# Layer-norm rows on ScalarE, mask operands padded to 128 rows, and 18 first-pass products moved between the down products of a two-FFN attention kernel

## What is computed

```python
x = x + 0.5 * _L0_ffn_ref(_layernorm(x), ...)
x = x + _L0_attn_ref(_layernorm(x), ...)
x = x + 0.5 * _L0_ffn_ref(_layernorm(x), ...)
```

## Time and profile before

| | us |
|---|---|
| median of 3 runs | 827.32 (825.87 to 828.84) |
| the profiled execution, its own time | 826.89 |
| its span, first to last instruction | 824.9 |
| PE busy | 753.1 (91%) |
| DVE busy | 592.5 (72%) |
| ACT busy | 431.5 (52%) |
| POOL busy | 69.7 (8%) |

### The profile page before, as it was taken

The page is one execution under the profiler, slowest core; times in us unless marked ns, Lnnn a source line. Parts: engine busy times, 40 slices in busy tenths (PEclk is TensorE's granted clock), DMA queues, the critical chain, the costliest instruction groups (busy, mean ns, idle before and its releaser), DMA issues.

```text
span 824.9 us, 15805 instructions
## 1 busy us (share of the span) xinstructions
PE 753.1 (91%) x5508; PEld 329.2 (40%) x5508; DVE 592.5 (72%) x1913; ACT 431.5 (52%) x626; POOL 69.7 (8%) x83
## 2 busy tenths in 40 slices
PE   3979998775799999999999999999998879899998
PEld 2623333332234344444444444444443655233343
DVE  4875332777899999999999999999993377433301
ACT  3432323333337687676876768767677434223211
POOL 2200000444400000000000000000000021000000
PEclk9979999999769999999999999999999989699999
DMA  4201000153401010110101101011000000000012
GB/s 128 67 0 15 0 1 0 49 160 95 133 13 34 20 34 18 34 35 22 32 18 35 34 21 32 18 35 35 22 14 2 1 1 1 0 1 0 0 39 64
DMA packets 33068, 26.08 MB, mean 32 GB/s; under 512 B 5707, under 2 KB 32331, under 8 KB 32997
## 3 DMA queue, kind: packets, MB, share of 16 engines
q1 hardware_dynamic: 32996, 25.15, 10.7%
HBM read 14.62 MB, written 10.26 MB: 30 GB/s over the span
## 4 chain that ended last, share of the span: by engine, by line
PE 63%; DVE 19%; issue 12%; ACT 3%; POOL 1%; SPq 0%; DMA 0%; DVEq 0%; ACTq 0%; POOLq 0%
PE ps L964 57%; DVE mx L853 8%; PE ps L969 5%; DVE xn L659 3%; DVE mx L846 1%; ACT h_all L580 1%; POOL rstd L421 1%; DVE stats L647 1%; PE ps L1012 1%; DVE x L802 1%; DVE h_all L846 1%; DVE mv L651 1%; DMA x<-in_x 0%; SPq L310 0%; DVE wb L874 0%
## 5 line engine op out<-in xcount | busy, mean ns | idle before, releaser
L580 ACT ACTIVATE h_all<-ps 128x1024 f32<-128x1024 f32 (+3 forms) x384 | 291.1, 811 | 118.4 <-PE ps L964 115.0
L853 DVE TENSOR_REDUCE mx<-ps 128x1 f32<-128x512 f32 (+2 forms) x352 | 222.6, 681 | 8.5 <-PE ps L964 5.9
L964 PE MATMUL ps<-ks,xnT_all 57*128 57x512 bf16 (+3 forms) x768 | 180.3, 336 | 10.7 <-DVE mx L846 5.3
L964 PE MATMUL ps<-h_all,vb 128*32 128x512 f32 (+3 forms) x1536 | 163.0, 498 | 0.6 <-ACT osb L569 0.6
L964 PE MATMUL ps<-xnT_all,ks 59*128 59x512 bf16 (+3 forms) x768 | 158.4, 330 | 3.7 <-ACT h_all L580 3.4
L846 DVE CUSTOM_DVE_ANT_0 h_all<-ps,mask_w 128x384 bf16<-128x384 f32 (+1 forms) x256 | 148.9, 618 | 2.1 <-issue 0.3
L670 DVE TENSOR_TENSOR h_all<-ps,sg 128x512 f32<-128x512 f32 (+1 forms) x80 | 55.1, 689 | 107.9 <-PE ps L964 71.3
L964 PEld LDWEIGHTS ps<-ks,xnT_all 57*128 57x128 bf16 x768 | 56.7, 94 | 141.3 <-DVE mx L846 66.1
L964 PE MATMUL ps<-cb 64*128 64x64 bf16 (+3 forms) x1216 | 111.8, 214 | 0.0
L495 ACT ACTIVATE sg<-ps 128x512 f32<-128x512 f32 x80 | 47.6, 598 | 106.3 <-PE ps L964 106.3
L964 PEld LDWEIGHTS ps<-cb 64*128 64x128 bf16 x1216 | 79.8, 96 | 16.7 <-issue 0.3
(11 more groups left out here) (123 smaller groups left out, 627.3 us busy)
## 6 DMA issues: line engine op xcount, KB each, us to landing
xnT_all<-q_scr SPq DMA_DIRECT2D x64, 96.0 KB
q_scr<-qp SPq DMA_DIRECT2D x8, 384.0 KB, 2.7
ks<-k_scr SPq DMA_DIRECT2D x64, 48.0 KB
x<-in_x SPq DMA_DIRECT2D x8, 256.0 KB, 2.9
q_scr<-qp SPq DMA_DIRECT2D x8, 256.0 KB, 2.9
out<-x SPq DMA_DIRECT2D x8, 256.0 KB, 2.3
xnT_all<-bias_scr SPq DMA_DIRECT2D x64, 18.0 KB
q_scr<-qp SPq DMA_DIRECT2D x8, 128.0 KB, 2.3
```

Source lines behind the costliest of these rows:

```text
L580: act.activation(pr[:, (NSTEP * i + s) % PR_BUFS, p:HPG:SLOTS, lo:HALF], ps[:, b:b + 2, lo:HALF], ACT.Exp)\
L853: dve.tensor_reduce(m, src, AX.X, V.max).then_inc(a_out, 1)
L964: return pe.matmul(o, l, r, start=start, stop=stop, skip_group_check=True)
```

## The change

What it does, by place:

- **Loads.** Group loads of x have a semaphore each and no longer wait for one another; group 1 goes ahead of the weights. `ident`, `gate_w`, `lb`, `rank` are issued from ACT's queue; the masks, `esel`, slopes and `qpos` are loaded behind x, ACT's copies of them (`constants`) run in front 6, and `slope_parts` behind `choose`.
- **Rows on ACT.** DVE only makes `shift` = -mean x rstd (one small operation, `ln_shift`); ACT applies scale and shift to the four tiles, in both FFNs' fronts and in the down stage. The copy into `xnT` in the fronts is gone.
- **Shared products.** Those of groups 4 to 7 are taken out of the fronts and put behind them, before the routed tiles; their `hidden` stand inside `choose`. The first `mask_T` stands ahead of the first two gate and up products.
- **Mask operands.** `esel` and `maskT` have 128 rows, 120 of them zero.
- **Down stage of the first FFN.** Banks: y 7, both turns 3, V 4, Q 5, K 6, and 0 to 2 for the ring. V is made directly with tokens on the rows (four products, bias on DVE); K comes as four products into one 128x128 block, and its split moves from POOL to DVE. `v_T` is gone. `EARLY` puts 2 first-pass products behind group 3's projection, and for groups 4 to 7 two before the last down product and two behind the projection: 18 in all. Group 7's split (`last_split`) is put behind product 21 of the first pass.
- **Stores.** k is stored by one DMA for each part and row: nine DMAs in place of six for each group. The first stack is loaded behind group 0's store, the first maxima ahead of group 7's.
- **Loops** over groups are written out on all engines.

The diff, cut to its core (`...` marks what is left out):

```diff
+EARLY = [(0, 0), (0, 0), (0, 0), (0, 2), (2, 2), (2, 2), (2, 2), (2, 2)]
+EARLY_END = sum(map(sum, EARLY))
+LAST_SPLIT = EARLY_END + 4
...
-def over_groups(eng, body):
...
+def over_groups(body):
+    for c in range(GROUPS):
+        body(c, c % 2, c == 0, c == GROUPS - 1)
...
-        esel = sb("esel", [EXPERTS, MT * P], BF16)
+        esel = sb("esel", [P, MT * P], BF16)
-        maskT = sb("maskT", [EXPERTS, 2, GN], BF16)
+        maskT = sb("maskT", [P, 2, GN], BF16)
...
+            sp.dma_start(xt(0), xd[0]).then_inc(s_x[0], 16)
+            sp.dma_start(xt(1), xd[1]).then_inc(s_x[1], 16)
             load(ffn_loads, s_w)
+            for c in range(2, GROUPS):
+                sp.dma_start(xt(c), xd[c]).then_inc(s_x[c], 16)
+            load(const_loads, s_const)
...
+                    for m in range(products):
+                        sp.dma_start(k_scr[b, :, r + m, n].rearrange("k (t n) -> t k n", t=GT), kp[:, par, m])\
+                            .then_inc(dw, 16)
...
+            def ln_apply(c, par, s_nm, s_T, s_xn):
+                act.wait_ge(s_nm, c + 1)
+                after(act, s_T, c)
+                for t in range(GT):
+                    ins = act.activation(xn[:, t, :], x[:, c * GT + t, :], ACT.Identity, bias=shift[:, par, t:t + 1],
+                                         scale=rstd[:, par, t:t + 1])
+                ins.then_inc(s_xn, 1)
...
                     act.activation(xnT_all[:, c, :], bank(7 * par), copy).then_inc(f.xA, 1)
-                    if not first:
+                    if not last:
+                        ln_apply(c + 1, 1 - par, f.nm, f.T, f.xn)
+                    if 0 < c <= LATE_SHARED:
                         silu(c - 1, 1 - par)
+                    if load_constants and c == GROUPS - 2:
+                        constants()
...
+                    act.activation(kp[:, par, 0, :], ps[:, 6, 0:P], ACT.Identity, bias=bk[:, 0:1])
+                    act.activation(kf[:, :], ps[:, 6, 0:P], ACT.Identity, bias=bk[:, 0:1]).then_inc(f.kf, 1)
...
+                dve.scalar_tensor_tensor(out=shift[:, par, :], in0=mv[:, par, :, 0], scalar=-1.0, in1=rstd[:, par, :],
+                                         op0=V.mult, op1=V.mult).then_inc(s_nm, 1)
...
+                    shared(LATE_SHARED)
+                    shared(LATE_SHARED + 1)
                     first_max(s2, m2, r2, pick2)
...
                     mask(0, 0)
+                    for c in range(LATE_SHARED + 2, GROUPS):
+                        shared(c)
...
                         ln_stats(c, par, ch, f.ve2)
-                        ln_apply(c, par, f.rs2, f.Tb, f.xn2)
+                        early_maxima(early(c, 0))
+                        ln_shift(c, par, f.rs2, f.xn2, f.nm2)
                         if not first:
                             split(c - 1, 1 - par)
+                            values(c - 1, (c - 1) // 2, 1 - par)
+                        early_maxima(early(c, 1))
...
+                def down(c, par, transpose=False):
+                    after(pe, f.yT, c if qkv else c - 1)
                     for i in range(HT):
                         if transpose and i == HT // 2 + 1:
                             xn_T(c - 2)
+                        if transpose and i == HT - 1:
+                            early_pieces(early(c - 1, 0))
...
                     mm(bank(5), wq[:, :], xnT[:, par, :]).then_inc(f.Q, 1)
+                    for t in range(GT):
+                        ins = mm(ps[:, 4, w * t:w * t + w], xnT[:, par, t * P:(t + 1) * P], wkv[:, w:2 * w])
+                    ins.then_inc(f.V, 1)
+                    after(pe, f.kf, c)
+                    for t in range(GT):
+                        ins = mm(ps[w * t:w * t + w, 6, 0:P], wkv[:, 0:w], xnT[:, par, t * P:(t + 1) * P])
+                    ins.then_inc(f.K, 1)
```

More of the change, by code:

```diff
@@ L84, with early @@
 BO_PARTS = 8
-EARLY = [range(0, 3), range(3, 9), range(9, 10)]
-START_T = HPG + 10
+LATE_SHARED = GROUPS - 4
+EARLY = [(0, 0), (0, 0), (0, 0), (0, 2), (2, 2), (2, 2), (2, 2), (2, 2)]
+assert len(EARLY) == GROUPS
+def early(c, k):
+    start = sum(map(sum, EARLY[:c])) + sum(EARLY[c][:k])
+    return range(start, start + EARLY[c][k])
+EARLY_END = sum(map(sum, EARLY))
+LAST_SPLIT = EARLY_END + 4
+assert FIRST_HALF <= early(GROUPS - 1, 1).start and LAST_SPLIT < NP1
 W1_STEP = 0
@@ L265, in macaron @@
         s_late = sem("s_late")
-        s_x0 = sem("s_x0")
+        s_const = sem("s_const")
+        s_x = [sem(f"s_x{c}") for c in range(GROUPS)]
         s_init = sem("s_init")
@@ L515, in routed_tiles @@
                             mask_T(c + 1, 1 - par)
-                over_groups(act, front)
-                silu(GROUPS - 1, 1)
+                ln_apply(0, 0, f.nm, f.T, f.xn)
+                over_groups(front)
                 act.wait_ge(f.lg, GROUPS)
                 act.activation(sc, lg, ACT.Sigmoid).then_inc(f.sig, 1)
+                for c in range(LATE_SHARED, GROUPS):
+                    silu(c, c % 2)
                 mask_T(0, 0)
-                over_groups(act, routed_tiles)
+                over_groups(routed_tiles)
             def ffn_down(f, qkv):
@@ L708, in choose, with shared @@
                 def choose():
+                    def shared(c):
+                        hidden(c, c % 2, c, MT)
                     dve.wait_ge(f.sig, 1)
@@ L878, in normalise, with early_maxima, attention @@
+            def early_maxima(some):
+                for n in some:
+                    reduce(0, n)
+                    if n == FIRST_HALF - 1:
+                        maxima(0, 0)
+            def attention(last_split):
                 def normalise(i, j):
@@ L942, in out_proj @@
                 residual(1, 1)
-                with dve.Fori(1, BATCH - 1) as b:
+                for b in range(1, BATCH - 1):
                     gather(2 * b + 2, b + 1, 0, 0)
@@ L1068, in body @@
+                    turn(lambda t: xn[:, t, :], 3).then_inc(f.Tb, 1)
                 def body(c, par, first, last):
                     if not last:
-                        down(c + 1, 1 - par, 0 if first or not qkv else 1 if isinstance(c, int) and c == 1 else 2)
+                        down(c + 1, 1 - par, qkv and not first)
                     pe.wait_ge(f.yT, c + 1)
-                    after(pe, f.x, c - 1)
-                    turn(lambda t: yT[:, par, t * P:(t + 1) * P], 2 + par).then_inc(f.T2, 1)
+                    after(pe, f.x, c if qkv else c - 1)
@@ L1074, in body @@
                     if qkv and last:
-                        v_T(c - 2)
                         xn_T(c - 1)
-                        pe.wait_ge(a_ld[0][0], 16 * LOADS)
-                        pe.wait_ge(s_ks0, 4)
-                        pe.wait_ge(f.x, GROUPS)
-                        for n in EARLY[0]:
-                            piece(0, n)
+                        early_pieces(early(c, 0))
+                    if qkv:
+                        after(pe, f.xTb, c)
+                    turn(lambda t: yT[:, par, t * P:(t + 1) * P], yT_bank(qkv, par)).then_inc(f.T2, 1)
```

352 lines of the change are left out of this document (156 added, 196 removed).

## The result

The changed kernel takes 804.62 us (803.68 to 805.79, 4 runs) against 827.25 for the kernel before in the same session: a ratio of 0.973 (0.970 to 0.975). The forecast was 804. The profiled execution took 804.09, its span is 802.2 against 824.9, so 22.7 us of span went.

The account below looks back on a forecast made before the run. TensorE, busy 91% of the span, was taken as the bound, waiting or running badly in some stages. From 826.9, FFN 1 -5.4, FFN 2 -6.3, down stage and tail -14.9 gave 800.3; clock made it 803.3, median 804, range 797 to 809.

Parts of the forecast that it names:

- the clock's 3.0: Both FFNs' fronts: TensorE may fall to the low clock in groups 5 to 7; 1.5 us put in for each.
- the down stage: First FFN: groups 8.3 us apart without early pieces, 9.3 with them; 64.0 against 62.75, so +1.3.
- the tail: From turn 7 to unit 0's last maximum, first FFN: 24.7 us where it was 40.9, so -16.2.
- Start: Constants leave the first wait, so DVE's statistics begin at 4.2 us instead of 8.91: -4.7.
- no saving: it makes a new loop: Fronts: ACT's rows, Silu, hidden, statistics and shift make 4.8 us a group; +4.6 in FFN 1, +3.5 in FFN 2.
- The padding: Routed tiles: mask operands of 128 rows save 0.30 us on each of 20 tiles, -6.0 in each FFN.
- rival 2: Routed tiles: padding gains nothing, 12.0 us at the counted tiles and 3 in the first ones gone: 819; chance 0.15.
- The order: Four shared products moved into `choose`, first routed tiles behind the mask turn: +0.7 us in FFN 1, -3.8 in FFN 2.
- Rival 1: The clock falls in both FFNs' fronts: +7 us over the forecast, 811; chance 0.14.
- Rival 3: Down stage: the 18 pieces do not come early, half the tail's gain is lost, 812; chance 0.09.
- Rival 4: Down stage: waits for xn let the clock fall for good, +7.2 us a group, 850; chance 0.04.
- Rival 5: The shift/scale loop is shorter (`ln_apply` 1.1), -0.5 us in some ten places, ring waits vanish: 794; chance 0.08.

Follow-up runs that it names:

- mask8: The changed kernel with esel and maskT back on 8 rows, without the 120 zero rows: 821.9 us, ratio 0.991.
- before_padded: The kernel before with one edit, esel and maskT on 128 rows, 120 of them zero: 806.7 us, ratio 0.975.
- shared_in_fronts: The changed kernel with the shared products of groups 4 to 6 back in the fronts, rows still on ACT: 806.7 us, ratio 0.975.
- tiles_first: The changed kernel with the fronts' rows on DVE, all shared products there, and the first two tiles' products ahead of the mask's turn: 786.9 us, ratio 0.951.
- stack1_late: The changed kernel with unit 1's twelve stack loads behind group 5's store instead of ahead of group 2's: 803.3 us, ratio 0.970.

## Why the prediction was right, point by point

**The time** was met, 804 for 804.6, and the sum of the stages too: 803.3, the clock's 3.0 included, against 804.1 in the profile. Each line of the table above has the forecast sign but the down stage, and none is off by more than 2.4. The mechanisms named were those found. Some luck is in it: the down stage was put 2.0 too long and the tail 2.4 too short, and the two cancel. What the sum did not show is how much two parts cost against the best place that they could have, because it compared each with the kernel before.

**Start.** Right: statistics at 4.32 for 4.2.

**Rows on ACT.** The price of four tiles was right, 1.65 for 1.6, and so was the step "no saving: it makes a new loop". The loop is 4.44 where I had 4.8 (from start to start, by the rows shown at the loop, 1.55, 0.68, 0.61, 1.40 and 0.20: neighbours overlap, and there is no wait of 0.2 beside the shift). What I did not ask was what the fronts would be without it. I compared with 34.9, the kernel before, which made two copies of xn; against DVE rows in the changed kernel the loop costs 6.7 and 7.0 us, where the sum shows 4.6 and 3.5.

**`choose` to the down stage.** The padding was priced right. The sum names 6.0 in each FFN, and rival 2 adds 3 for the padded tiles inside the layouts: 15 in all. Between mask8 and the changed kernel these stages differ by 7.3 and 8.0. The order was right too once its clock is counted: +0.7 and -3.8, with 1.5 each for the padded tiles in them taken out (half of rival 2's 3) and 1.5 each for the clock put in, are +3.7 and -0.8 without padding; mask8 measured +3.9 (86.7 against 82.8) and 0.0 (85.1 both). What I did not ask is what padding is worth in the old order: 9.1 and 11.8. Against the old order with padding the new one loses 5.8 and 3.8, and a comparison with the kernel before can't show that.

**Which part did it.** I gave the tail and down stage 14.9 of the gain and the padding 12, or 15 with its first tiles. Padding alone brings 21.7 in the kernel before, to 806.7, and the rest of the change, with 14 us won in the down stage and tail and 3.5 at the start, adds about 2 us, which its interval can't tell from nothing, since the same change gives back some 16 us in the two FFNs (fronts 6.2, stretch behind `choose` 9.6, against before_padded).

**Rival 1, the clock.** It fell in the last fronts of both FFNs as feared (35.17, 1.11 for a turn). shared_in_fronts, which gives TensorE more work and a higher clock there, wins nothing; what the low clock costs apart from the loop is not shown. *Rival 2* is refuted by both padding runs. *Rival 3*: the pieces came early and are worth 8.5, with the stack in time. *Rival 4*, slower: the clock stayed up until turn 6 of 7; in mask8 and tiles_first it fell in the first group and came back. *Rival 5*: the rows on ACT took 1.65, not 1.1.

**Down stage.** 8.18 for 8.3 without pieces, 9.0 for 9.3 with them. Groups 5 to 6 took 10.24, and I had looked at the landing of the first stack, not at what unit 1's loads hold up behind them on SP. That a queue that I had checked for one consumer delays another is the part of the sum that was missing, though small here (0.5). In the kernel without early products it was 5.

**Tail.** 27.1 for 24.7. The projection of group 7 ran at half speed:

```profile
201.50 2.07 PE L991 MATMUL ps<-xnT,wq 128*128 128x512 f32 x2 [0.69 <-ACT xnT L553]
...
205.15 0.29 DVE L826 TENSOR_TENSOR v_all<-ps,bv 128x128 f32<-128x128 f32 x1 [3.35 <-PE ps L991]
```

and DVE, which has the products' maxima behind its `values` of this group, waited 3.35 for it. I had that work at the full clock. In mask8 and stack1_late this product took 1.35, the wait was 2.17 and the tail 25.9, so the half speed is about 1.2 of the 2.4 missed; the rest is open.

**Sums.** Added up again, TensorE's terms for a group with pieces give 9.5 instead of 9.3, those of the tail 24.3 instead of 24.7, and seven groups of rival 4 come to 854 instead of 850. None of this changes the forecast.

## What to carry to other kernels

A sum can come out right and still not show which part is worth having: undo the parts one by one, above all those that the sum calls cheap. Here one small part, zero rows in an operand so that all of TensorE's blocks in a routed tile have one size, carried the gain, and a part that moved work to the idler engine cost 15 us by closing a loop through it. Compare a moved step with the best place it could have in the new kernel, not with the old kernel; and where an in-order queue gets new entries, ask of each one who stands behind it.

## What the runs showed of the hardware

- The load of a weight block that differs in size from the float32 128x128 block before it waits 0.76 us instead of 0.24, whether the block is short of rows (8x128) or of columns (128x8, 128x64). For the 8x128 block this costs 0.30 us a tile: with 128 rows, zeros included, the tile fell from 2.23 to 1.93. For the other two sizes the cost was not measured.
- Three operations of 32x512 on POOL (1.15 each) made four tiles on DVE take 3.79 instead of 1.11. On DVE the same three take 0.67 each.
- A row-wise scale and bias of a 128x128 tile on ACT takes 1.65 for four, against 1.11 on DVE.
- In the second FFN's fronts of the changed kernel, where TensorE waits for ACT's rows in most groups, the mean granted clock was 0.70 (644 to 683 us); with rows on DVE it was 0.79 (636 to 668 us).
